# Keeping the rows that routed results are added to in SBUF, and stepping through pages of 128 rows four at a time

## What is computed

```python
h = tok(x, ...)                      # causal decayed mean over 32 positions, then two 256x256 matmuls
h = h + attn(layernorm(h), ...)      # 16 heads of 16, causal softmax over 375 positions
flat = layernorm(h)                  # and the FFN on it, added to h:
out = sum over 2 shared experts of (silu(flat @ wg_s) * (flat @ wu_s)) @ wd_s       # 128 wide each
probs = softmax(flat @ router_w)     # 16 routed experts
weights, indices = top_k(probs, 2);  weights /= weights.sum + 1e-9
out += sum over the 2 chosen e of weights[e] * (silu(flat @ wg_r[e]) * (flat @ wu_r[e])) @ wd_r[e]   # 64 wide
```

## The time and the profile before

| | |
|---|---|
| median of 3 runs | 2279.42 us |
| profiled execution: time / span | 2266.05 / 2264.2 us |
| granted TensorE clock, mean over the span | 0.924 |
| TensorE matmul busy | 1926.4 us, 85% |
| VectorE (DVE) busy | 1389.1 us, 61% |
| ScalarE (ACT) busy | 975.7 us, 43% |
| GpSimd (POOL) busy | 955.4 us, 42% |
| moved by DMA | 336.44 MB, 149 GB/s over the span |

### The profile page before, as it was taken

The page is one execution under the profiler, slowest core; times in us unless marked ns, Lnnn a source line. Parts: engine busy times, 40 slices in busy tenths (PEclk is TensorE's granted clock), DMA queues, the critical chain, the costliest instruction groups (busy, mean ns, idle before and its releaser), DMA issues. The chain is left out here.

```text
span 2264.2 us, 49922 instructions
## 1 busy us (share of the span) xinstructions
PE 1926.4 (85%) x14553; PEld 1414.7 (62%) x14554; DVE 1389.1 (61%) x3745; ACT 975.7 (43%) x2082; POOL 955.4 (42%) x1315
## 2 busy tenths in 40 slices
PE   4899999999999999999999875887887859767773
PEld 3677767777776777777777643554554558656663
DVE  3367777778787877777787734555555523344333
ACT  1155565656565656556565542222222224233221
POOL 3033444444444434444444342555555422545445
PEclk7599999999999999999999976999999979889887
DMA  2234444444444444444443425444443347878786
GB/s 64 63 111 139 127 131 126 135 124 133 123 136 121 128 130 123 136 126 133 123 136 111 130 62 149 142 145 143 147 147 138 115 142 236 280 261 289 251 268 223
DMA packets 244050, 336.44 MB, mean 149 GB/s; under 512 B 46358, under 2 KB 182266, under 8 KB 243962
## 3 DMA queue, kind: packets, MB, share of 16 engines
q1 hardware_dynamic: 158234, 224.23, 31.0%
q10 hardware_dynamic: 67680, 61.87, 10.0%
q0 software_dynamic: 18048, 49.31, 6.7%
HBM read 109.99 MB, written 148.31 MB: 114 GB/s over the span
## 5 line engine op out<-in xcount | busy, mean ns | idle before, releaser
L793 DVE TENSOR_REDUCE neg_max<-bank 120x1 f32<-120x376 f32 (+2 forms) x896 | 526.0, 596 | 261.9 <-PE bank L585 251.5
L718 ACT ACTIVATE probs<-bank 128x376 f32<-128x376 f32 (+2 forms) x896 | 453.8, 522 | 307.1 <-PE bank L603 302.4
L571 PE MATMUL bank<-k_rows,q_rows 64*128 64x128 f32 (+2 forms) x1536 | 429.8, 352 | 53.4 <-DVE neg_max L793 26.2
L603 PE MATMUL bank<-q_rows,k_rows 64*120 64x120 f32 (+2 forms) x1536 | 393.5, 341 | 4.8 <-ACT probs L718 3.0
L571 PEld LDWEIGHTS bank<-k_rows,q_rows 64*128 64x128 f32 (+1 forms) x1536 | 240.1, 189 | 209.9 <-DVE neg_max L793 67.5
L904 POOL TENSOR_SCALAR_AFFINE_SELECT probs<-probs 128x512 f32<-128x512 f32 (+1 forms) x384 | 233.9, 629 | 283.0 <-ACT probs L718 283.0
L2050 POOL DMA_INDIRECT y_got<-y_sorted,p_route x188 | 180.5, 960 | 238.5 <-DMA p_base<-base_dram 78.4
L585 PE MATMUL bank<-causal,own_row 64*120 64x120 bf16 (+4 forms) x1792 | 279.1, 237 | 0.0
L1702 POOL DMA_INDIRECT x_sorted<-r_normed,route x188 | 183.3, 975 | 197.2 <-DVE route L1558 145.5
L603 PEld LDWEIGHTS bank<-q_rows,k_rows 64*128 64x128 f32 (+1 forms) x1536 | 224.4, 186 | 10.2 <-ACT probs L718 5.6
L585 PEld LDWEIGHTS bank<-causal,own_row 64*128 64x128 bf16 (+2 forms) x1792 | 179.9, 118 | 28.4
(11 more groups left out here) (203 smaller groups left out, 3893.2 us busy)
## 6 DMA issues: line engine op xcount, KB each, us to landing
x_sorted<-zeros ACTq DMA_DIRECT2D x32, 880.0 KB, 6.2
y_sorted<-zeros ACTq DMA_DIRECT2D x32, 880.0 KB, 7.9
x_rows<-x_sorted SPq DMA_DIRECT2D x55, 512.0 KB
y_sorted<-p_y_rows SPq DMA_DIRECT2D x55, 512.0 KB
q_rows<-q_flat_hi SPq DMA_DIRECT2D x256, 94.0 KB
k_rows<-k_flat_hi SPq DMA_DIRECT2D x256, 94.0 KB
q_rows<-q_flat_lo SPq DMA_DIRECT2D x128, 94.0 KB
k_rows<-k_flat_lo SPq DMA_DIRECT2D x128, 94.0 KB
```

The lines of the kernel that those rows point to most:

```text
L571: eng.matmul(ps[0:T[t], m * w:(m + 1) * w], q[rows, slot, t * P:t * P + T[t]], k[rows, slot, 0:w], start=(m == 0), stop=False, skip_group_ ...
L603: last = eng.matmul(ps[0:T[t], m * w:(m + 1) * w], k[64 * c:64 * c + 64, slot, t * P:t * P + T[t]], q[64 * c:64 * c + 64, slot, t * P:S], ...
L718: eng.activation(probs[g % 2][0:T[t], first:first + len(heads), OFF[t]:OFF[t] + w], bank_exp[n % 2][0:T[t], 0:len(heads) * w].rearrange("k ...
L793: eng.tensor_reduce(dst, src, AX.X, ALU.max, negate=True).then_inc(max_taken, 1)
```

## The change

- Pages have 128 rows in place of 256: 204 pages (26112 rows), four a step, 51 steps (`FOURS`). A group may give up to four new pages to an expert, so `count_pages` runs three times a group, and `pass_pages` twice, since the table has up to 256 entries in two columns; it is stored by two DMAs.
- `base` is one tile of 128 x 94 x 256 in SBUF (96 KB a partition), kept from the routing to the end. The h2 rows are loaded straight into it, and ACT and DVE read them there, at an address from the loop's register. `load_base`, `store_base` and `base_dram` go.
- In the pages `combine` adds in place in base, two steps after the gather (`USED`), and after `keep_y`. `AHEAD`, `LAG` are 5, 7. x has four buffers and is loaded five steps ahead, in rows of 1 KB; y_got has four; hT and its bank have two. A step's order is, on TensorE, hidden_T, gate_up, transposes, down, and then one register load of four expert numbers; on ACT keep_hT, tanh, keep_xT twice, keep_y; on SP load_x, load_route, store_y, store_result.
- `clear_pages` writes from a tile of 128 x 816 zeros, two runs a partition, 835 KB a DMA, in place of 80 partitions of 11 runs of 1 KB, 880 KB.

The diff, cut (the shapes of tiles, semaphores and renamed loops are left out):

```diff
         pages = (2 * self.B * self.S + self.E * (self.PAGE - 1)) // self.PAGE
-        self.PAGES = pages + pages % 2
+        self.PAGES = pages + -pages % 4
...
-                    n = sh.PAGES * sh.PAGE // (B * 80)
-                    eng.dma_start(rows.rearrange("(b p r) d -> b p r d", b=B, p=80)[st.b + 2 * st.i],
-                                  zeros[0:80, :].rearrange("p (r d) -> p r d", r=1).broadcast_to([80, n, D]))\
+                    cleared = rows.rearrange("r d -> (r d)").rearrange("(b p a c) -> b p a c", b=B, p=P, a=2)
+                    eng.dma_start(cleared[st.b + 2 * st.i],
+                                  zeros[:, :].rearrange("p (a c) -> p a c", a=1).broadcast_to([P, 2, FILL]))\
                         .then_inc(pages_cleared, 16)
...
+    def rows_of(st, shift, first, n):
+        return base[:, bass.ds(st.at(shift, TILES, first), n), :]
...
-                        eng.wait_ge(base_loaded[par], st.turn(-1, 2, 16, 16))
                         eng.wait_ge(down_done, st.at(-1, 1, 1))
-                    rows = base[par][:, 2 * half:2 * half + 2, :].rearrange("p t d -> p (t d)")
+                    rows = rows_of(st, -1, 2 * half, 2).rearrange("p t d -> p (t d)")
                     last = eng.tensor_tensor(rows, bank_y[half][:, 0:2 * D], rows, ALU.add)
...
+                def count_pages(st, more):
+                    eng.scalar_tensor_tensor(out=new_pages[:, :], in0=beyond[:, :], scalar=float(more * PAGE),
+                                             in1=(grows if more == 1 else new_pages)[:, :],
...
+                def pass_pages(st, n):
+                    eng.scalar_tensor_tensor(out=passed[:, n, :], in0=given[st.b % 2][:, :], scalar=page_no[:, n:n + 1],
+                                             in1=passed[:, n, :], op0=ALU.is_le, op1=ALU.add).then_inc(state_step, 1)
...
-                        count_pages(st)
+                        count_pages(st, 1)
                         divisor(st)
+                        count_pages(st, 2)
+                        invert(st)
+                        count_pages(st, 3)
                         give_pages(st)
-                        invert(st)
...
-                        pass_pages(st)
+                        pass_pages(st, 0)
+                        pass_pages(st, 1)
...
-                    eng.dma_start(h2[par][:, 0:tiles(st, shift), :], h2_rows(st, shift)).then_inc(h2_loaded[par], 16)
-                def load_base(st):
-                    par = (st.b + 1) % 2
-                    if not st.before(1, 2):
-                        eng.wait_ge(base_stored[par], st.turn(1, 2, 16))
-                    eng.dma_start(base[par][:, 0:tiles(st, 1), :], h2_rows(st, 1)).then_inc(base_loaded[par], 16)
-                def store_base(st):
-                    par = (st.b - 1) % 2
-                    wait_alone(eng, y_read, st.at(-1, 1, 1), passed_sp)
-                    eng.dma_start(base_rows(st, -1), base[par][:, 0:tiles(st, -1), :]).then_inc(base_stored[par], 16)
+                    eng.dma_start(rows_of(st, shift, 0, tiles(st, shift)), h2_rows(st, shift))\
+                        .then_inc(h2_loaded[(st.b + shift) % 2], 16)
...
-                    if st.runs(-1, GROUPS):
-                        store_base(st)
-                    if st.runs(1, GROUPS):
-                        load_base(st)
...
-                eng.dma_start(page_dram, page_expert[:, :]).then_inc(pages_stored, 16)
-                eng.wait_ge(pages_stored, 16)
+                for n in range(2):
+                    eng.dma_start(page_dram[n], page_expert[:, n:n + 1]).then_inc(pages_stored, 16)
+                eng.wait_ge(pages_stored, 32)
...
-    AHEAD, LAG = 9, 11
+    AHEAD, LAG = 5, 7
+    USED = LAG + 2
-    def pair_rows(rows):
-        return rows.rearrange("(q a p t) d -> q p a (t d)", a=2, p=P, t=2)
...
+    def base_of(st, shift, first, n):
+        return base[:, bass.ds(st.at(shift, 2, first), n), :].rearrange("p t d -> p (t d)")
...
-        x_rows = [sb(f"x_rows{p}", [P, 2, 2 * D]) for p in range(2)]
+        x_rows = [sb(f"x_rows{p}", [P, 4, D]) for p in range(RING)]
...
-        hT = sb("hT", [P, 2 * P])
+        hT = [sb(f"hT{p}", [P, 2 * P]) for p in range(2)]
...
-        base = [sb(f"p_base{p}", [P, 2 * D]) for p in range(4)]
-        y_got = [sb(f"y_got{p}", [P, 2, 2, D]) for p in range(2)]
-        first = sb("first", [P, 2, D])
-        result = [sb(f"result{p}", [P, 2 * D]) for p in range(2)]
+        y_got = [sb(f"y_got{p}", [P, 2, 2, D]) for p in range(4)]
...
+                def load_experts(st):
+                    eng.reg_load(expert_no[st.b % 2], page_row[0:1, bass.ds(st.at(2, 4), 4)])
...
-                    if st.runs(1, PAIRS):
+                    if st.runs(0, FOURS):
+                        hidden_T(st)
+                    if st.runs(1, FOURS):
                         gate_up(st)
-                    if st.runs(0, PAIRS):
-                        hidden_T(st)
-                    if st.runs(2, PAIRS):
+                    if st.runs(2, FOURS):
                         transposes(st)
-                    if st.runs(0, PAIRS):
+                    if st.runs(0, FOURS):
                         down(st)
+                    if st.runs(2, FOURS):
+                        load_experts(st)
...
-                    shift = -1 - LAG
-                    par, ring = (st.b + shift) % 2, (st.b + shift) % 4
-                    eng.wait_ge(batch_loaded[ring], st.turn(shift, 4, 32, 32))
-                    eng.wait_ge(y_gathered[par], st.turn(shift, 2, 64, 64))
+                    shift = -USED
+                    ring = (st.b + shift) % 4
+                    eng.wait_ge(route_loaded[ring], st.turn(shift, 4, 16, 16))
+                    eng.wait_ge(y_gathered[ring], st.turn(shift, 4, 64, 64))
                     for t in range(2):
-                        if t == 0 and not st.before(shift, 1):
-                            eng.wait_ge(result_done, st.at(shift))
-                        eng.scalar_tensor_tensor(out=first[:, t, :], in0=y_got[par][:, t, 0, :],
+                        eng.scalar_tensor_tensor(out=base_of(st, shift, t, 1), in0=y_got[ring][:, t, 0, :],
                                                  scalar=route[ring][:, 4 * t + 2:4 * t + 3],
-                                                 in1=base[ring][:, t * D:(t + 1) * D],
-                                                 op0=ALU.mult, op1=ALU.add).then_inc(first_done, 1)
-                    if not st.before(shift, 2):
-                        eng.wait_ge(result_stored[par], st.turn(shift, 2, 16))
+                                                 in1=base_of(st, shift, t, 1), op0=ALU.mult, op1=ALU.add)\
+                            .then_inc(first_done, 1)
                     for t in range(2):
                         eng.wait_ge(first_done, st.at(shift, 2, t + 1))
-                        last = eng.scalar_tensor_tensor(out=result[par][:, t * D:(t + 1) * D], in0=y_got[par][:, t, 1, :],
+                        last = eng.scalar_tensor_tensor(out=base_of(st, shift, t, 1), in0=y_got[ring][:, t, 1, :],
                                                         scalar=route[ring][:, 4 * t + 3:4 * t + 4],
-                                                        in1=first[:, t, :], op0=ALU.mult, op1=ALU.add)
+                                                        in1=base_of(st, shift, t, 1), op0=ALU.mult, op1=ALU.add)
                     last.then_inc(result_done, 1)
                 def step(st):
-                    if st.runs(1, PAIRS):
+                    if st.runs(1, FOURS):
                         gated_of(st)
                         hidden_of(st)
-                    if st.runs(-1 - LAG, BATCHES):
+                    if st.runs(0, FOURS):
+                        keep_y(st)
...
-                    wait_alone(eng, batch_loaded[ring], st.turn(shift, 4, 32, 32), passed_pool)
-                    if not st.before(shift, 2):
-                        wait_alone(eng, result_done, st.at(shift - 1), passed_pool)
+                    wait_alone(eng, route_loaded[ring], st.turn(shift, 4, 16, 16), passed_pool)
+                    if not st.before(shift, 4):
+                        wait_alone(eng, result_done, st.at(shift - 3), passed_pool)
...
-                            eng.indirect_dma_start(y_got[par][:, t, k, :], None, y_sorted, at)\
-                                .then_inc(y_gathered[par], 16)
+                            eng.indirect_dma_start(y_got[ring][:, t, k, :], None, y_sorted, at)\
+                                .then_inc(y_gathered[ring], 16)
...
-                    par = (st.b + shift) % 2
-                    if not st.before(shift, 2):
-                        wait_alone(eng, T_done, st.at(shift - 2, 2, 2), passed_sp)
-                    eng.dma_start(x_rows[par][:, :, :], x_pairs[st.at(shift)]).then_inc(x_loaded[par], 16)
+                    ring = (st.b + shift) % RING
+                    if not st.before(shift, RING):
```

(34 more changed lines are left out.)

204 lines of the change are left out of this document (103 added, 101 removed).

## The result

The changed kernel takes 2241.93 us (median of four, 2236.7 to 2248.93) against 2277.87 of the kernel before (2272.94 to 2291.36): a ratio of 0.985, interval 0.980 to 0.989. The medians lie 36 us apart.

What follows compares the result with a forecast made beforehand. Steps with gathers were taken as bound by DMA bytes and by TensorE completions held during long gather runs. Terms -19.3 - 40 - 5 + 6 + 7 = -51: 2215 us profiled, 2228 median, range 2185 to 2272.

Steps and rivals of the forecast that it cites:

- holds stay: Rival, pages: GpSimd's own gather runs delay TensorE's completions whatever the buffers; 9 to 13 holds, sum -17, 2262 us; chance 0.24.
- I keep 5 of the 10 holds: Pages: five holds (TensorE's completion delayed by long gather runs) remain, 5.6 us each; 43.5 steps at 6.0 us; -40.
- I am wrong if: Conditions: gather runs of eight stay or lengthen, route waits replace p_base's 76 us, or routing moves over 10 us.
- the runs merge: Slower rival, pages: pauses between gather runs get too short, every second step held, 20 holds; +33, 2312 us; chance 0.11.
- Bytes: Pages, steps with gathers: 0.875 of the bytes gives 5.5 us, 1 KB runs up to 10% more, 6.1; 6.0 taken.
- Fewer steps: Pages: 51 steps for 55, gathers start at step 7 not 11; four steps of 4.82 us without gathers go; -19.3.
- Routing: Routing: less base traffic 0; second pass_pages and two run-time-address results cost 0.25 us a group; +6, bounds -10 to +24.
- the page table: Page table's store as two DMAs of 128 4-byte runs: +8.4 us if they follow each other, +1 if overlapping; +7 taken.
- The end: Program's end: keep_y ahead of the combine lets DVE keep the last y rows earlier, opening the last gathers; -5 us.
- Fills: Clearing the pages, 835 KB a step for 880 in longer runs, beside TensorE at 96%: 0.
- my fastest case: Rival, pages: the added buffering removes every delay of TensorE's completions and routing costs nothing; -85, 2194 us; chance 0.17.
- the slack: Pages: more x and y_got buffers, earlier x loads and a combine two steps after its gather absorb late transfers.

Runs made afterwards that it cites:

- lag11: Changed kernel with AHEAD, LAG back at 9, 11, so the first gather comes four steps later; ratio 0.994 to the kernel before, pages' time 401.7 us.
- steps55: Changed kernel with 16 empty pages more, so 55 steps, gathers' start unchanged; ratio 0.990 to the kernel before, pages' time 405.8 us.
- used8: Changed kernel with the combine one step after its gather instead of two, on the third chip; ratio 0.972 to the kernel before, pages' time 330.5 us.
- plain_dma: Changed kernel with GpSimd's four indirect gathers replaced by plain DMAs of fixed rows; 2123.58 us, ratio 0.927 to the kernel before.

## Why the prediction was right and where it was not

The measured 2241.93 lies 14 us above my 2228, inside the range, with the sign I forecast. That is in part luck. In the profiled executions, on which the sum was made, I forecast -51 us and the trace has -26, half of it. I then added 13 us for the distance from the profiled execution to the median, which for the changed kernel was 2 us, and that brought the forecast nearer. Step by step it is the mechanism of the rival *holds stay* that the trace shows, and its -17 us is nearer to the -26 than my -51; only in the medians does its 2262 lie further off than my 2228.

*The step that failed* is the one on the holds: "I keep 5 of the 10 holds", and with it 6.0 us a step. The stretch with gathers was to lose 40 us; it lost 6. The tanh's remote waits rose from ten to 18, the holds of 3 us or more from eight to 13. The rival said why: the cause is GpSimd's own gathers, and as many have to be issued whatever the buffers. I had read from one run of eight and one run of four that only long runs hold. That was wrong too: three of the eight holds of the kernel before and five of the 13 of the changed one lie beside no run longer than four. In ten of the 13 the tanh starts 1.3 to 3.1 us after a run has ended, in the other three inside a run, up to 7.6 us before its end. The form of the sum fails with it: 18 waits at 5.6 us beside 6.0 us a step would have made 362 us, where 328 were measured. (By the sum itself the change is slower than before from 15 holds on and by over 1% from 19, not from 14 and 18 as I wrote.) Two of the conditions that I wrote down as "I am wrong if" came true: runs of gathers grew from eight to twelve, and a route load of 4 KB took over the waits of the 256 KB base load, 73 us after 76. A part of *the runs merge* came true as well: held steps got more frequent. The steps with gathers under 7 us, which I take as undisturbed, changed little: their median is 5.6 us, where the kernel before has 5.8, and eight of them are at 4.6 or 4.7.

*Bytes.* I took the time of an undisturbed step as proportional to its bytes. With the base traffic put back the pages' time did not rise, and with a quarter of the gathers' bytes it did not fall. On the chips with holds the term has no size that can be seen. No run takes the 1 KB runs of x and y by themselves; ahead of the gathers the DMA engines have a share of 0.63 at 201 GB/s, where they had 0.61 at 200, some 3% more for the same bytes and not 10%.

*Fewer steps*: forecast -19.3, and the stretch without gathers lost 22.3. The size was right. The sum gave all of it to the earlier first gather; lag11 and steps55 suggest that the fewer steps have a part in the gain too, and don't settle how large.

*Routing* and *the page table*: forecast +6 and +7, measured +1.5 and +0.4. The path through DVE was as I had it, but the price was not. The two pass_pages take

```profile
1569.54 0.38 DVE L1499 SCALAR_TENSOR_TENSOR passed<-given,page_no,passed 128x16 f32<-128x16 f32 x2
```

where one took 0.23, and the results at a run-time address take 0.68 us each, as before; from the gating to the slots this step has 5.35 us in place of 5.20, so 0.15 us a group where I had 0.25. The two stores overlap (landing after 6.3 and 7.6 us, where one alone took 8.4). The Trainium skill makes the fit that I set beside them, in "DMA: Bandwidth & Descriptors", from DMAs that GpSimd issues, and these are SP's; its 2 us is not what the trace shows for either. For the table I had taken nearly the upper bound, for the routing the middle; the 11 us that did not come made up for a third of the 34 us that the stretch with gathers fell short.

*The end*: forecast -5, measured +2.9. DVE does keep its half of the last y rows within 1 us of ACT's, but 15 gathers still start behind the last y, where the kernel before had twelve.

*Fills*: 0 was forecast, and the 2.5 us ahead of the first logits are within what executions differ by. In one unit the fills are 816 KB in place of 880, so the traffic that I gave as 3 MB is 4.2 MB; with a forecast of 0 nothing hangs on it.

What I did not have among my cases is that the answer depends on the chip. On the third chip the change is worth 4.9%, more than my fastest case, with not one hold. There the slack does what I described: used8 puts 38 us of the pages on the combine's second step. The step also reached the time to which I had given no weight: the Trainium skill, "DMA: Bandwidth & Descriptors", "Specifications", gives 358 GB/s to a core's HBM traffic, from which I had worked out 5.1 us a step as an estimate; the trace of that chip has 5.14 us a step, which agrees, but at 338 GB/s, which is less, and plain_dma with 370 is above the page's figure.

## What to carry to other kernels

When GpSimd issues indirect DMAs beside a pipeline of TensorE, compare the end of a matmul with the start of its reader. A reader that starts microseconds later, with a remote releaser and mostly just after a run of gathers has ended, is not waiting for data; here neither fewer bytes nor another order of the step moved it. Make GpSimd wait inside its run for the pipeline it disturbs: that took 37 us off the pages here. Where there was nothing to win, it cost, together with the split scatters, some 8 us. And run the same kernel on a second chip before a term is believed: which of two limits a stage has can change with it.

## What the runs showed of the hardware

- On two chips TensorE's completions reach ACT and DVE late while GpSimd issues indirect DMAs: 12.6 us late beside a run of twelve, 6 us beside a run of four. ACT's reach DVE within 0.33 us in the same trace. On a third chip with the same kernel TensorE's reach the tanh within 0.04 us beside a run of sixteen. What sets the chips apart is not in the traces.
- Indirect DMAs with a quarter of the bytes hold as much (13 holds, 75.4 us, beside 13 and 80.1). Plain DMAs from GpSimd, at 0.54 us each and with as many packets and bytes, hold nothing.
- Between a chip with holds and the one without, the same kernel differs by 391.1 - 292.3 = 98.8 us in the pages and 436.2 - 354.7 = 81.5 us in the routing; TensorE's granted clock in the stretch with gathers is 0.84 beside 0.98. In the pages plain_dma, which has no hold on a chip with holds, supports that the holds are the cause; for the routing it is not shown.
- Two small stores issued one behind the other landed after 6.3 and 7.6 us; they did not add up.
- The DMA engines moved 370 GB/s in the stretch with gathers of plain_dma (share 1.05).
